# Wide attention: probabilities scaled on GpSimd before the transposes, one step later, in place of spreading the reciprocal sums through TensorE

## Chip, core and metric

The kernel runs on one core of one Trainium2 chip. The metric is the device time of one execution in microseconds (us), and the median of several executions is what counts. The engines are TensorE (PE; its weight loads are listed apart as PEld), VectorE (DVE), ScalarE (ACT), GpSimd (POOL) and SyncE (SP).

## Reference

The whole program is a network of 16 layers, each added to its input `x` of shape (4, 512, 128) after a layer norm. The change touches one of them, the wide attention `L1b`, with 16 heads of size 64 and `D` = 128:

```
q = einsum('bnd,hde->bhne', query, Wq) / sqrt(64)
k = einsum('bmd,hde->bhme', query, Wk)
v = einsum('bmd,hde->bhme', query, Wv)
attn = softmax(einsum('bhne,bhme->bhnm', q, k), axis=-1)
out = einsum('bhnm,bhme->bnhe', attn, v)
out = swapaxes(out, -1, -2).reshape(B, N, E * H)
x = x + dot(out, Wp) + bp
```

All of it is float32.

## The kernel before

A loop on the chip runs twice, each time over two batch rows (`NB` = 2) of 512 tokens (`T`), through all 16 layers. So `wide_attention` (L1446 on) runs twice in one execution. `x` lies with features on the partitions.

**Tiling.** A unit `u` is one batch row and one pair of heads: `UN` = 16 units. A step `s = 4u + t` is a tile of 128 queries of a unit, for both heads of the pair: `STEPS` = 64. PSUM has eight banks of 128x512: banks 0 to 3 take scores (two per step, alternating), bank 4 the transposes of head 0, bank 5 those of head 1, bank 6 (`SMALL`) projections, the spread sums and the output in turn, bank 7 (`PV`) the sum of the products of a unit.

**One step.** TensorE computes the scores of two heads (`scores`, L1502). VectorE takes the row maxima (`maxima`, L1635) and negates them (L1637, a 128x2 operation from SBUF to SBUF, `mneg`). ScalarE takes the exponential of each head with the row sum as a by-product (`exps`, L1598; a second short record reads the accumulator) into `pr`. TensorE turns the 128x512 probabilities of each head in four 128x128 transposes (`turn`, L1513), and VectorE (head 0, L1661) and ScalarE (head 1, L1623) copy them to `prt`. Once a unit's four steps are turned, `products(u, j)` (L1525) multiplies v by `prt`, one `j` in each step of the next unit.

**The normalisation.** After the fourth step of a unit VectorE takes the reciprocal of the eight sums (L1666, `inv`). TensorE spreads them over the partitions with eight small matmuls against the identity (`denominators`, L1536) into bank 6, ScalarE copies them to `invb` (`take_spread`, L1606), and VectorE multiplies bank 7 by `invb` into `at` (`normalise`, L1643). After eight units `output` (L1545) multiplies `at` by `Wp`: 16 records of TensorE, after which VectorE adds the result to `xs` (L1648).

**Order.** Every engine has its own instruction stream in program order, written out by hand, with semaphores between them. In step `s` TensorE runs `scores(s+1)`, `products(u-1, t)`, at t = 0 `denominators(u-1)` (and in unit 9 `output(0)`), at t = 1 to 3 one projection of unit u+2 (`project`, L1488 for k and q, L1491 for v), and `turn(s)`. The last two units have no projections left. VectorE runs `maxima(s+1)`, the copy of head 0 of step `s`, and at t = 3 the reciprocal and `normalise(u-1)`. ScalarE runs `exps(s+1)`, at t = 0 `take_spread(u-1)`, at t >= 1 the copy of a projection (`take`), and the copy of head 1. GpSimd has no work in this layer. `products(u, 0)` waits for the copies of step 4u+3 by both engines and, through `at_ready`, until bank 7 has been read for unit u-1.

Of the kernel before, what the change touches and what calls it, by code (L numbers as in the profile page):

```python
# [5 lines left out]
P = 128  # L6
BATCH = 4
T = 512
# [3 lines left out]
KT = T // P  # L12
# [5 lines left out]
HE = 64  # L18
# [5 lines left out]
ALU = mybir.AluOpType  # L24
# [1422 lines left out]
def wide_attention(g, name):  # L1447
# [5 lines left out]
    with Stage(g, name) as st:  # L1453
# [4 lines left out]
        pr = st.sb("pr", [P, 2, 2, T])  # L1458
# [3 lines left out]
        total = st.sb("total", [P, 2, KT, 2])  # L1462
        inv = st.sb("inv", [P, 2, KT, 2])
        invb = st.sb("invb", [P, T])
# [3 lines left out]
        inverse, spread, spread_in, pv, at_ready, out_ready, added = (  # L1468
            st.sem(n) for n in ("inverse", "spread", "spread_in", "pv", "at_ready", "out_ready", "added"))
        SMALL, PV = 6, 7  # L1470

        with g.nc.Block() as block:
# [5 lines left out]
            def _(pe):  # L1478
                ln.tensor(pe)

                def project(u, j):
# [3 lines left out]
                    if u >= 3 and j == 0:  # L1485
                        pe.wait_ge(spread_in, u - 2)
# [19 lines left out]
                def turn(s):  # L1506

                    for h in range(2):
                        pe.wait_ge(prob, 2 * s + h + 1)
                        if s >= 1:  # L1510
                            pe.wait_ge((turned_dve, turned_act)[h], s)
                        for j in range(KT):
                            mm = pe.transpose(g.ps[:, 4 + h, j * P:(j + 1) * P], pr[:, s % 2, h, j * P:(j + 1) * P], g.w("ident"))  # L1513
# [16 lines left out]
                def denominators(u):  # L1530

                    pe.wait_ge(inverse, u + 1)
                    pe.wait_ge(proj_in, min(3 * (u + 3), 3 * UN))
                    for t in range(KT):
                        for h in range(2):
                            mm = pe.matmul(g.ps[HE * h:HE * h + HE, SMALL, t * P:(t + 1) * P], widen(inv[:, u % 2, t, h:h + 1], HE), g.w("ident"),  # L1536
                                           start=True, stop=True, skip_group_check=True)
                    mm.then_inc(spread, 1)

                def output(b):  # L1540

                    pe.wait_ge(at_ready, PAIRS * (b + 1))
                    pe.wait_ge(spread_in, min(PAIRS * (b + 1) + 1, UN))
# [9 lines left out]
                for s in range(STEPS):  # L1553
# [3 lines left out]
                    if u >= 1:  # L1557
                        products(u - 1, t)
                    if t == 0 and u >= 1:
                        denominators(u - 1)  # L1560
                        if u % PAIRS == 1 and u > 1:
                            output(u // PAIRS - 1)
# [4 lines left out]
                    turn(s)  # L1567
                denominators(UN - 1)
# [5 lines left out]
            def _(act):  # L1574
# [14 lines left out]
                def exps(s):  # L1589

                    u, t = s // KT, s % KT
                    act.wait_ge(max_in, s + 1)
                    if t == 0 and u >= 2:
                        act.wait_ge(inverse, u - 1)
# [548 lines left out]
```

## Time and profile before

| what | us |
|---|---|
| median of three runs | 3803.88 (3800.67 to 3805.98) |
| the profiled execution | 3797.76 |
| its span | 3796.1 |

| engine | busy us in the whole span | share |
|---|---|---|
| PE | 2777.9 | 73% |
| DVE | 1910.9 | 50% |
| ACT | 1454.2 | 38% |
| POOL | 563.0 | 15% |

The layer `L1b` lies between about 639 and 929 us of the span, and in the second pass of the loop between about 2523 and 2813 us. A row of the timeline gives the start in us from the start of the span, the duration in us, the engine, the line, the operation, output <- input, the shapes and how often it stands there in a row; in square brackets is the idle time ahead of it and what ended it. Float32 matmuls are recorded as two instructions each.

### The profile page before, as it was taken

The page shows a single profiled execution, that of the slowest core. Times are in us where ns is not written, and L with a number is a line of the kernel's source. Part 1 is how long each engine was busy: PE and PEld are TensorE (multiplying, and loading weights), DVE is VectorE, ACT ScalarE, POOL GpSimd, SP SyncE. Part 2 cuts the span into 40 slices and gives each one's busy share as a digit, 9 for nine tenths or more (in the row PEclk, how much of TensorE's full clock was granted, in tenths as well). Part 3 has the DMA queues.
Part 4 walks back from the last instruction along what each step waited for, and adds up shares of the span by engine and source line. Part 5 has one row for each costly group of instructions (what it writes and reads, how often), then busy time and mean ns, then how long its engine had stood idle before and what let it go on. Part 6 is the DMA issues. An engine that isn't in the chain of part 4 may idle for free. (4 is left out here: it accounts for less than half of the span.)

```text
span 3796.1 us, 33099 instructions
## 1 busy us (share of the span) xinstructions
PE 2777.9 (73%) x11584; PEld 1230.2 (32%) x11630; DVE 1910.9 (50%) x2675; ACT 1454.2 (38%) x2370; POOL 563.0 (15%) x376
## 2 busy tenths in 40 slices
PE   3565778999695797573846567889996957965647
PEld 1221164544342343131212212635443423422312
DVE  4858642554315613872549575425533166148635
ACT  2442412654242444432434334036542423434323
POOL 0532000000014010430006400000000140105300
PEclk8897969999797998895969889599997979988969
DMA  2001000000011110002000020000000011100010
GB/s 85 0 1 42 10 1 1 1 1 1 6 39 30 23 45 0 0 3 20 1 12 0 0 44 8 1 1 1 1 1 28 17 34 18 45 0 0 9 14 6
DMA packets 103312, 52.11 MB, mean 14 GB/s; under 512 B 75232, under 2 KB 91616, under 8 KB 103136
## 3 DMA queue, kind: packets, MB, share of 16 engines
q1 hardware_dynamic: 103136, 49.88, 5.6%
q8 instruction: 96, 1.57, 0.2%
q14 instruction: 80, 0.66, 0.1%
HBM read 40.02 MB, written 9.44 MB: 13 GB/s over the span
## 5 line engine op out<-in xcount | busy, mean ns | idle before, releaser
L1598 ACT ACTIVATE L1b_pr<-ps,L1b_mneg 128x512 f32<-128x512 f32 x256 | 173.5, 683 | 196.1 <-DVE L1b_mneg L1637 196.1
L518 POOL TENSOR_TENSOR xs<-xs,L2f_part 128x512 f32<-128x512 f32 x32 | 40.5, 1265 | 1286.6 <-DVE L2f_part L507 1286.6
L1635 DVE TENSOR_REDUCE L1b_m<-ps 128x2 f32<-128x1024 f32 x128 | 156.8, 1225 | 104.9 <-PE ps L1502 100.8
L1356 ACT ACTIVATE L0b_pt<-ps 128x1024 f32<-128x1024 f32 x128 | 129.5, 1023 | 208.6 <-PE ps L1294 206.7
L90 ACT ACT_TABLE_LOAD x32 | 41.1, 1283 | 423.3 <-PEq L671 180.5
L1403 DVE TENSOR_REDUCE L0b_mx<-ps 128x1 f32<-128x512 f32 x256 | 161.3, 685 | 46.8 <-PE ps L1278 38.9
L1046 POOL TENSOR_TENSOR L0a_db<-L0a_du,L0a_bs 128x1024 f32<-128x1024 f32 x64 | 150.3, 2353 | 224.4 <-ACT L0a_bs L1017 213.7
L1046 POOL TENSOR_TENSOR L3a_db<-L3a_du,L3a_bs 128x1024 f32<-128x1024 f32 x64 | 150.3, 2352 | 224.6 <-ACT L3a_bs L1017 214.1
L1356 ACT ACTIVATE L2b_pt<-ps 128x1024 f32<-128x1024 f32 (+3 forms) x128 | 88.5, 703 | 204.8 <-PE ps L1297 204.3
L1278 PE MATMUL ps<-L0b_ks,L0b_qs 128*128 128x512 bf16 x246 | 100.7, 446 | 87.8 <-DMA L0b_ks<-parts_dram 51.9
L1661 DVE COPY L1b_prt<-ps 128x512 f32<-128x512 f32 x128 | 88.6, 692 | 124.8 <-PE ps L1513 124.5
L1122 DVE TENSOR_TENSOR_SCAN L0a_hs<-ps,L0a_db 128x1024 f32<-128x1024 f32 x64 | 146.1, 2283 | 10.0 <-ACT ps L1009 8.0
L1122 DVE TENSOR_TENSOR_SCAN L3a_hs<-ps,L3a_db 128x1024 f32<-128x1024 f32 x64 | 146.1, 2283 | 9.5 <-ACT ps L1009 8.0
L1502 PE MATMUL ps<-L1b_k,L1b_q 64*128 64x512 f32 x512 | 144.0, 640 | 0.0
L1403 DVE TENSOR_REDUCE L2b_mx<-ps 128x1 f32<-128x128 f32 (+3 forms) x256 | 116.8, 486 | 53.7 <-PE ps L1281 52.2
L116 PE MATMUL ps<-xs,weights 128*128 128x512 f32 x128 | 82.6, 780 | 78.9 <-PEq L220 27.2
L1525 PE MATMUL ps<-L1b_prt,L1b_v 128*64 128x512 f32 x512 | 136.7, 614 | 4.1 <-issue 2.0
L1513 PE MATMUL ps<-weights,L1b_pr 128*128 128x128 f32 x1024 | 135.8, 275 | 3.0 <-ACT L1b_pr L1598 3.0
L1513 PEld LDWEIGHTS ps<-weights,L1b_pr 128*128 128x128 f32 x1024 | 115.6, 141 | 50.6 <-issue 43.5
L1278 PE MATMUL ps<-L2b_ks,L2b_qs 128*128 128x256 bf16 (+3 forms) x242 | 74.8, 343 | 77.4 <-DMA L2b_ks<-parts_dram 50.9
L946 PE MATMUL ps<-L0a_hc,weights 128*128 128x512 f32 x256 | 127.7, 623 | 2.7 <-DVE L0a_hc L1127 2.7
L946 PE MATMUL ps<-L3a_hc,weights 128*128 128x512 f32 x256 | 127.4, 622 | 2.7 <-DVE L3a_hc L1127 2.7
(567 smaller groups left out, 5787.8 us busy)
## 6 DMA issues: line engine op xcount, KB each, us to landing
L2f_w<-expert_dram SPq DMA_DIRECT2D x32, 256.0 KB, 3.0
L2g_w<-expert_dram SPq DMA_DIRECT2D x32, 256.0 KB, 3.1
weights<-w_dram SPq DMA_DIRECT2D x7, 789.5 KB, 8.8
parts_dram<-L0b_cut SPq DMA_DIRECT2D x4, 768.0 KB, 3.3
L0b_qs<-parts_dram SPq DMA_DIRECT2D x96, 32.0 KB
L0b_ks<-parts_dram SPq DMA_DIRECT2D x96, 32.0 KB
parts_dram<-L2b_cut SPq DMA_DIRECT2D x4, 768.0 KB, 3.3
L2b_qs<-parts_dram SPq DMA_DIRECT2D x96, 32.0 KB
```

The costliest lines, as they stand in the source:

```text
L946: mm = pe.matmul(g.ps[:, k, :], g.w("ident"), hc[:, n % 2, k, :], start=(s == 0), stop=(s == NS - 1))
L1046: pool.tensor_tensor(db[:, n % 2, :, :], du[:, b, :, :], bcast(bs[:, n % 2, :], 1, 2), ALU.mult).then_inc(input_ready, 1)
L1122: dve.tensor_tensor_scan(flat(hs), decay_banks(n).rearrange("p k t -> p (k t)"), flat(db), 0.0, ALU.mult, ALU.add).then_inc(scanned, 1)
L1278: mm = pe.matmul(g.ps[:, 4 + a % 2, 0:span(t)], qs[:, b, i, r, t * P:(t + 1) * P], ks[:, b, i, r, 0:span(t)], start=True, stop=not causal)
L1356: act.activation(pt[:, n % 3, 2 * half:2 * half + 2, q0:T], g.ps[:, 2 * (s % 2):2 * (s % 2) + 2, q0:T], ACT.Exp).then_inc(prob, 1)
L1403: dve.tensor_reduce(mx[:, u, n:n + 1], g.ps[:, 4 + a % 2, 0:span(n % 4)], AX.X, ALU.max).then_inc(top_in, 1)
L1502: mm = pe.matmul(g.ps[:, 2 * (s % 2) + h, :], q[HE * h:HE * h + HE, u % 3, t * P:(t + 1) * P], k[HE * h:HE * h + HE, u % 3, :], start=True ...
L1513: mm = pe.transpose(g.ps[:, 4 + h, j * P:(j + 1) * P], pr[:, s % 2, h, j * P:(j + 1) * P], g.w("ident"))
L1525: mm = pe.matmul(g.ps[HE * h:HE * h + HE, PV, :], v[:, u % 4, j, HE * h:HE * h + HE], prt[:, u % 2, h, j, :], start=(j == 0), stop=(j == K ...
L1598: act.activation(pr[:, s % 2, h, :], g.ps[:, 2 * (s % 2) + h, :], ACT.Exp, bias=mneg[:, s % 2, h:h + 1], accum_out=total[:, u % 2, t, h:h ...
L1635: dve.tensor_reduce(m[:, s % 2, :], g.ps[:, 2 * (s % 2):2 * (s % 2) + 2, :], AX.X, ALU.max).then_inc(max_raw, 1)
L1661: dve.tensor_copy(prt[:, u % 2, 0, :, t * P:(t + 1) * P], g.ps[:, 4, :].rearrange("p (j c) -> p j c", c=P)).then_inc(turned_dve, 1)
```

## The change

`denominators`, `take_spread`, `normalise`, the tile `invb` and the semaphores `spread` and `spread_in` go. In their place:

- VectorE takes the reciprocal of a step's two sums in every step (`invert`), 128x2 in place of 128x8.
- GpSimd multiplies the probabilities of each head by that reciprocal, in place, in SBUF: two `tensor_scalar` of 128x512 in every step, which raise `normal`.
- `turn` waits for `normal` and no longer for `prob`, and is run one step later: `turn(s-1)` in step `s`, at the end of the step. `pr` has three buffers for it. `products` go one step later as well, so `products(u-1, 0)` stands in step 4u+1. `output` goes from t = 0 to t = 1, ahead of `project`.
- `take_at(u)` on VectorE copies bank 7 to `at` in place of `normalise`. It stands at t = 0 of unit u+2, behind `invert(s+1)`.
- `total` and `inv` alternate by step, `exps(s)` waits for `inverse` of two steps before.

```diff
-        pr = st.sb("pr", [P, 2, 2, T])
+        pr = st.sb("pr", [P, 3, 2, T])
...
# TensorE
                 def turn(s):
                     for h in range(2):
-                        pe.wait_ge(prob, 2 * s + h + 1)
+                        pe.wait_ge(normal, 2 * s + h + 1)
...
-                def denominators(u):
-                    pe.wait_ge(inverse, u + 1)
-                    pe.wait_ge(proj_in, min(3 * (u + 3), 3 * UN))
-                    for t in range(KT):
-                        for h in range(2):
-                            mm = pe.matmul(g.ps[HE * h:HE * h + HE, SMALL, t * P:(t + 1) * P], widen(inv[:, u % 2, t, h:h + 1], HE), g.w("ident"),
-                                           start=True, stop=True, skip_group_check=True)
-                    mm.then_inc(spread, 1)
...
                     if s + 1 < STEPS:
                         scores(s + 1)
-                    if u >= 1:
-                        products(u - 1, t)
-                    if t == 0 and u >= 1:
-                        denominators(u - 1)
-                        if u % PAIRS == 1 and u > 1:
-                            output(u // PAIRS - 1)
+                    if s >= 1 + KT:
+                        products((s - 1) // KT - 1, (s - 1) % KT)
+                    if t == 1 and u > 1 and u % PAIRS == 1:
+                        output(u // PAIRS - 1)
                     if t >= 1 and u + 2 < UN:
                         if t == 1 and u > 1 and u % PAIRS == 1:
                             pe.wait_ge(added, u // PAIRS)
                         project(u + 2, t - 1)
-                    turn(s)
-                denominators(UN - 1)
+                    if s >= 1:
+                        turn(s - 1)
+                products(UN - 2, KT - 1)
+                turn(STEPS - 1)
                 for j in range(KT):
                     products(UN - 1, j)
                 output(NB - 1)
# ScalarE
                     act.wait_ge(max_in, s + 1)
+                    if s >= 2:
+                        act.wait_ge(inverse, s - 1)
...
                     if s + 1 < STEPS:
                         exps(s + 1)
-                    if t == 0 and u >= 1:
-                        take_spread(u - 1)
                     if t >= 1 and u + 2 < UN:
                         take(u + 2, t - 1)
...
+                    if s >= 1:
+                        take_turned(s - 1)
+                take_turned(STEPS - 1)
# GpSimd
+                for s in range(STEPS):
+                    pool.wait_ge(inverse, s + 1)
+                    for h in range(2):
+                        pool.tensor_scalar(pr[:, s % 3, h, :], pr[:, s % 3, h, :], inv[:, s % 2, h:h + 1], None, ALU.mult).then_inc(normal, 1)
# VectorE
+                def invert(s):
+                    dve.wait_ge(prob, 2 * s + 2)
+                    if s >= 2:
+                        dve.wait_ge(normal, 2 * (s - 1))
+                    dve.reciprocal(inv[:, s % 2, :], total[:, s % 2, :]).then_inc(inverse, 1)
...
+                def take_at(u):
                     dve.wait_ge(pv, u + 1)
-                    dve.tensor_tensor(at[:, u // PAIRS % 2, u % PAIRS, :], g.ps[:, PV, :], invb[:, :], ALU.mult).then_inc(at_ready, 1)
+                    dve.tensor_copy(at[:, u // PAIRS % 2, u % PAIRS, :], g.ps[:, PV, :]).then_inc(at_ready, 1)
...
                 maxima(0)
+                invert(0)
                 for s in range(STEPS):
                     u, t = s // KT, s % KT
                     if s + 1 < STEPS:
                         maxima(s + 1)
-                    if t == 0 and u > 1 and u % PAIRS == 1:
+                    if t == 1 and u > 1 and u % PAIRS == 1:
                         output(u // PAIRS - 1)
+                    if s >= 1:
+                        take_turned(s - 1)
+                    if s + 1 < STEPS:
+                        invert(s + 1)
                     if t == 0 and u >= 2:
+                        take_at(u - 2)
...
+                take_at(UN - 2)
+                take_turned(STEPS - 1)
+                take_at(UN - 1)
                 output(NB - 1)
```

## Rows read from the trace of the kernel before

**Rows 1.** The page's first part: busy us, share and instructions of each engine.

```profile
PE 2777.9 (73%) x11584; PEld 1230.2 (32%) x11630; DVE 1910.9 (50%) x2675; ACT 1454.2 (38%) x2370; POOL 563.0 (15%) x376
```

**Rows 2.** Windows, layer `L1b`, first pass: window, us; PE, PEld, DVE, ACT, POOL; PEclk.

```profile
646.00:929.00 283.00, 271.75 (x1504) 135.88 (x1502) 145.62 (x226) 156.08 (x384) 0.00 (x0) 1.00 0.00 1
```

**Rows 3.** Timeline, a step with a projection (t = 1), 787.7 to 791.8 us.

```profile
787.78 1.13 PE L1502 MATMUL ps<-L1b_k,L1b_q 64*128 64x512 f32 x4
...
788.84 1.08 PE L1525 MATMUL ps<-L1b_prt,L1b_v 128*64 128x512 f32 x4
...
790.81 1.04 PE L1513 MATMUL ps<-weights,L1b_pr 128*128 128x128 f32 x8
...
791.45 0.69 DVE L1661 COPY L1b_prt<-ps 128x512 f32<-128x512 f32 x1 [1.06 <-PE ps L1513]
...
791.78 1.13 PE L1502 MATMUL ps<-L1b_k,L1b_q 64*128 64x512 f32 x4
```

**Rows 4.** Timeline, the step ahead of it (t = 0, with `denominators`), 783.7 to 787.8 us.

```profile
783.70 1.13 PE L1502 MATMUL ps<-L1b_k,L1b_q 64*128 64x512 f32 x4
...
784.09 0.64 DVE L1643 TENSOR_TENSOR L1b_at<-ps,L1b_invb 128x512 f32<-128x512 f32 x1
...
784.84 0.23 PEld L1525 LDWEIGHTS ps<-L1b_prt,L1b_v 128*64 128x64 f32 x4 [0.84 <-DVE L1b_prt L1661]
...
784.88 1.23 DVE L1635 TENSOR_REDUCE L1b_m<-ps 128x2 f32<-128x1024 f32 x1
...
785.75 1.07 PE L1536 MATMUL ps<-weights,L1b_inv 128*64 128x128 f32 x16
...
786.14 0.17 DVE L1637 TENSOR_SCALAR L1b_mneg<-L1b_m 128x2 f32<-128x2 f32 x1
786.34 0.69 ACT L1598 ACTIVATE L1b_pr<-ps,L1b_mneg 128x512 f32<-128x512 f32 x1 [1.61 <-DVE L1b_mneg L1637]
...
786.76 1.09 PE L1513 MATMUL ps<-weights,L1b_pr 128*128 128x128 f32 x8
...
787.59 0.20 ACT L1598 ACTIVATION_READ_ACCUMULATOR L1b_pr<-ps,L1b_mneg 128x1 f32 x1
```

**Rows 5.** Timeline, a step of the last units, with no projection: two `scores` in turn.

```profile
896.05 1.13 PE L1502 MATMUL ps<-L1b_k,L1b_q 64*128 64x512 f32 x4
...
899.14 1.13 PE L1502 MATMUL ps<-L1b_k,L1b_q 64*128 64x512 f32 x4
```

**Rows 6.** Timeline, `output(0)` in unit 9 and what follows it.

```profile
804.52 7.10 PE L1545 MATMUL ps<-L1b_at,weights 128*128 128x512 f32 x16 [1.59 <-ACT L1b_invb L1606]
...
811.46 1.04 PE L1513 MATMUL ps<-weights,L1b_pr 128*128 128x128 f32 x8
...
811.66 0.75 DVE L1648 SCALAR_TENSOR_TENSOR xs<-ps,weights,xs 128x512 f32<-128x512 f32 x1 [9.25 <-PE ps L1545]
```

**Rows 7.** Timeline, the layer's end: `scores(61)`, the last four `products`, the last addition.

```profile
902.23 1.13 PE L1502 MATMUL ps<-L1b_k,L1b_q 64*128 64x512 f32 x4
...
916.38 3.60 PE L1525 MATMUL ps<-L1b_prt,L1b_v 128*64 128x512 f32 x16
...
928.02 0.75 DVE L1648 SCALAR_TENSOR_TENSOR xs<-ps,weights,xs 128x512 f32<-128x512 f32 x1 [7.23 <-PE ps L1545]
```

**Rows 8.** Single lines on GpSimd, min/median/max in ns, first and last start.

```profile
L518 POOL TENSOR_TENSOR xs<-xs,L2f_part x32: 1260/1264/1270, 1063.3 to 3051.2; 128x512 f32<-128x512 f32 x32
...
L1375 POOL COPY L0b_vpad<-L0b_v x4: 396/858/1386, 304.1 to 306.6; 128x256 f32<-128x256 f32 x4
...
L1370 POOL MEMSET L0b_vpad<- x4: 524/524/524, 302.9 to 2188.0; 128x512 f32 x4
```

**Rows 9.** Timelines of GpSimd and VectorE in layer `L0b`, 284 to 309 us.

```profile
284.13 7.35 POOL L1365 MEMSET L0b_qs<- 128x8192 bf16 x1
...
285.92 6.11 DVE L1393 CAST L0b_cut<-L0b_ln_xc 128x1024 bf16<-128x1024 f32 x1
...
308.55 0.69 DVE L1397 CAST L0b_cut<-L0b_ln_xc 128x1024 bf16<-128x1024 f32 x1
```

More of the change, by code:

```diff
@@ L1461, in wide_attention @@
         mneg = st.sb("mneg", [P, 2, 2])
-        total = st.sb("total", [P, 2, KT, 2])
-        inv = st.sb("inv", [P, 2, KT, 2])
-        invb = st.sb("invb", [P, T])
+        total = st.sb("total", [P, 2, 2])
+        inv = st.sb("inv", [P, 2, 2])
         at = st.sb("at", [P, 2, PAIRS, T])
@@ L1467, in wide_attention @@
             st.sem(n) for n in ("proj", "proj_in", "score", "max_raw", "max_in", "prob", "turned", "turned_dve", "turned_act"))
-        inverse, spread, spread_in, pv, at_ready, out_ready, added = (
-            st.sem(n) for n in ("inverse", "spread", "spread_in", "pv", "at_ready", "out_ready", "added"))
+        inverse, normal, pv, at_ready, out_ready, added = (
+            st.sem(n) for n in ("inverse", "normal", "pv", "at_ready", "out_ready", "added"))
         SMALL, PV = 6, 7
@@ L1484, in project @@
                     pe.wait_ge(proj_in, 3 * u + j)
-                    if u >= 3 and j == 0:
-                        pe.wait_ge(spread_in, u - 2)
                     if j < 2:
@@ L1592, in exps, with take_turned @@
                     act.wait_ge(max_in, s + 1)
-                    if t == 0 and u >= 2:
-                        act.wait_ge(inverse, u - 1)
-                    for h in range(2):
-                        if s >= 2:
-                            act.wait_ge(turned, 2 * (s - 2) + h + 1)
-                        act.activation(pr[:, s % 2, h, :], g.ps[:, 2 * (s % 2) + h, :], ACT.Exp, bias=mneg[:, s % 2, h:h + 1],
-                                       accum_out=total[:, u % 2, t, h:h + 1]).then_inc(prob, 1)
-                def take_spread(u):
-                    act.wait_ge(spread, u + 1)
-                    if u >= 1:
-                        act.wait_ge(at_ready, u)
-                    act.activation(invb[:, :], g.ps[:, SMALL, :], ACT.Copy).then_inc(spread_in, 1)
+                    if s >= 2:
+                        act.wait_ge(inverse, s - 1)
+                    for h in range(2):
+                        if s >= 3:
+                            act.wait_ge(turned, 2 * (s - 3) + h + 1)
+                        act.activation(pr[:, s % 3, h, :], g.ps[:, 2 * (s % 2) + h, :], ACT.Exp, bias=mneg[:, s % 2, h:h + 1],
+                                       accum_out=total[:, s % 2, h:h + 1]).then_inc(prob, 1)
+                def take_turned(s):
+                    u, t = s // KT, s % KT
+                    act.wait_ge(turned, 2 * s + 2)
+                    if t == 0 and u >= 2:
+                        act.wait_ge(pv, u - 1)
+                    act.activation(prt[:, u % 2, 1, :, t * P:(t + 1) * P], g.ps[:, 5, :].rearrange("p (j c) -> p j c", c=P), ACT.Copy).then_inc(turned_act, 1)
                 for u in range(2):
```

31 lines of the change are left out of this document (11 added, 20 removed).

## The prediction

> **What bounds the kernel now.** I began with the page's busy shares: TensorE works 73% of the span, GpSimd 15% [rows 1]. Over the whole program that says little, since the change sits in one layer, so the second view was the windows of that layer. There TensorE is busy 271.75 of 283 us at a granted clock of 1.00 (its 2.4 GHz level), VectorE 146, ScalarE 156, GpSimd not at all [rows 2]. The layer is bound by TensorE's stream, and the same holds in the second pass. The third view was the timeline of one unit. A step with a projection lasts 787.78 to 791.78, 4.00 us, and TensorE goes from one group to the next without a wait [rows 3]. The step at t = 0 lasts 783.70 to 787.78, 4.08 us, of which 784.84 - 783.70 - 1.06 = 0.08 is a wait for the copies (1.06 is the spacing of `scores` and `products`, 787.78 to 788.84) [rows 3, 4]. A unit is thus about 16.1 us, and 16 units a pass give most of the 283 us.
>
> So work taken off TensorE's stream is worth its full length, but only as long as no wait takes its place. Where the other engines then stand has to be read at the step that is shortened.
>
> **What is removed from TensorE.** `denominators` takes the stream from 785.75 to 786.76, 1.01 us, once a unit [rows 4]. Sixteen a pass and two passes would be 32 us if nothing else came. The steps without a projection show the group `scores`, `products`, `turn` alone: 3.09 us [rows 5]. So the new step at t = 0 takes 3.09 us of work, and the other three stay at 4.00.
>
> **What TensorE then waits for.** Let 0 be the start of `scores(4u+1)`, in the step at t = 0. The next scores start at 3.09, and `products(u-1, 0)`, which the change puts behind them, could start at 3.09 + 1.06 = 4.15. It waits for `at_ready` of unit u-2, since it writes bank 7 anew. That is `take_at(u-2)`, and on VectorE it is queued behind `invert(4u+1)`, which waits for both exponentials of step 4u+1. The chain from 0, all on ScalarE and VectorE: the reduction starts at 1.18 (784.88 - 783.70), the negation at 2.44, the first exponential at 2.64, and the last accumulator read ends at 787.79, that is 4.09 [rows 4]. The reciprocal follows at 4.13 or so (the exponential starts 0.03 after the negation's end, 786.31; I take the same hand-over). Before it is a 128x8 operation followed at 0.11 us by the next on VectorE; that spacing I take for the 128x2 one. `take_at` starts at about 4.24 and lasts 0.64 to 0.69, as the multiply it replaces [rows 4] and the copy of the same size [rows 3]. With 0.05 for the hand-over TensorE can go at 4.96. That is a wait of 4.96 - 4.15 = 0.81 us in each unit. ScalarE's copy of the turned head 1, the other thing that `products(u-1, 0)` waits for, is done by 4.09 + 0.60, so it is not the last.
>
> Of 1.01 + 0.08 = 1.09 us, then, 0.81 comes back as the wait; with the small differences in spacing (4.08 + 1.06 to `products(u-1, 1)` before, 4.96 after) the gain is 5.14 - 4.96 = 0.18 us a unit. This is the step on which the forecast rests.
>
> **Whether a second wait forms.** VectorE is busy until 4.9 with `take_at`, so the maxima of step 4u+2, whose scores were there at 3.09 + 1.18 = 4.27, start 0.6 late and their exponentials end near 7.8. The next that needs them is `scores(4u+4)`, at 7.9 + 4.0; covered. The copies of the turned probabilities have over 1 us of cover. GpSimd: it gets step s at 4.09 + 0.2 after `scores(s)` and must be ready when `turn(s)` starts, a whole step later, at about 10.9 (`turn(4u+1)`). With duration p for each of the two, 4.4 + 2p < 10.9 holds for p below 3.2, and its throughput, 8p < 15.9 a unit, for p below 2.0. In the last two units, steps of 3.09, p must stay below 1.5.
>
> **The duration p** is not in the trace: there is no GpSimd `tensor_scalar`. Below stands the write alone, MEMSET of the same size, 0.524; above, the two-input TENSOR_TENSOR of the same size, 1.264. The nearest in kind reads one input and writes one output, the COPY of 128x256, 0.396 undisturbed, which doubled is 0.79 with its fixed part counted twice [rows 8]. I take 0.6 to 0.8, and keep 0.52 to 1.27. The Trainium skill, "GPSIMD Engine Reference", section Engine selection, says that one-input operations run at about line rate there; by that p would be at the low end of this range.
>
> **The other parts, one pass.** Start: the first maxima are held back by `invert(0)`, but `project` waits for ScalarE there already; worked through with the same durations, the seventh scores come 0.1 us later (0 to +1). Units 2 to 8 and 10 to 13, eleven of them: 11 x -0.18 = -2.0. Unit 9: the 1.59 us that `output(0)` waits for `invb` goes; in its place `project` stands right behind the output and waits for VectorE's addition, 811.66 - 811.46 + 0.75 + 0.05 = 1.0 us [rows 6], where a `turn` and more lay between before. So -0.6, and -0.18 as in the others: -0.8. Unit 14: -0.2. Unit 15 and the end: counted from `scores(61)`, the first products start at 4.96 and then come turn 60, scores 63, products, turn 61, products, turn 62, products, with spacings of 1.01 to 1.06, so that `turn(63)` starts at 13.15. Its 1.1 us, the ScalarE copy of 0.6 and hand-overs put the last four products at 15.05, where they start at 916.38 - 902.23 = 14.15 now [rows 7]. From there to the last addition all is as before. So +0.9. Off the path: 48 more reciprocals on VectorE, 16 copies fewer on ScalarE, both covered by TensorE.
>
> Sum: 0.1 - 2.0 - 0.8 - 0.2 + 0.9 = -2.0 a pass, two passes -3.9 us. The profiled execution, 3797.76 us with a span of 3796.1, would become 3793.9. It lies 6.1 below the median of the runs, so the forecast in terms of the median is 3803.9 - 3.9 = 3800.
>
> **Rival 1, slower: GpSimd holds up VectorE's negation.** The trace has it in another layer: a VectorE cast from SBUF to SBUF, 0.69 us when GpSimd is idle, took 6.11 us when it met a GpSimd MEMSET, and ended at 292.03, 0.55 after the MEMSET's end at 284.13 + 7.35 = 291.48 [rows 9]. It waited the instruction out. The negation `mneg` also goes from SBUF to SBUF with one input, and it is in the chain above. At t = 0 it comes at 2.44. GpSimd gets step 4u when `invert(4u)` is done. That one stands behind the copy that ends at 791.45 + 0.69 - 787.78 = 4.36 in its step [rows 3], i.e. at 0.36 of this one, so GpSimd starts at about 0.57 and ends at 0.63 + 2p. With p below 0.90 it is over by 2.44 and costs nothing. With p = 1.26 it ends at 3.15, and the negation ends near 3.26 in place of 2.61: 0.65 us in each of 14 waits a pass, 28 x 0.65 = 18 us, net +14, 3818. From p = 1.15 on it is slower by more than 0.2%. Against it: the COPY row; for it: no row shows a `tensor_scalar` as fast as a COPY. Chance 0.22, at any strength. The Trainium skill states this as a rule ("SBUF — State Buffer", section Who interferes with whom): a one-source VectorE operation in a two-port mode and a GpSimd instruction exclude each other for the whole instruction, whoever comes first; "Vector Engine (DVE) Microarchitecture Reference", section 5.1, adds that two elements a partition suffice. By that rule the trace agrees for the cast; for 128x2 no row shows it.
>
> **Rival 2, faster: the wait is not there.** If `take_at` were not last, all of the 1.01 us would be kept: 28 x 0.81 = 23 more, 27 in all, 3777. Against it stand the program order and the measured chain. Chance 0.10.
>
> **Rival 3: GpSimd becomes the bound**, from p = 2.0. With p = 2.35, a far price, a unit takes 18.8, 2.7 more than now, 28 x 2.7 = +75, 3879. Chance 0.05; the layer's TENSOR_TENSOR of 1.264 speaks against it.
>
> **How the numbers follow.** The forecast has 0.63. Its own range, from 0 to +1 at the start, 0.64 or 0.69 for the copy, 0.1 either way in the hand-overs (28 x 0.1 = 2.8) is 3795 to 3804. The range that should hold 8 in 10 goes up to rival 1 at p = 1.27, 3820, and leaves out rivals 2 and 3: 3794 to 3820. This kernel can be told from no change at about 0.2%, 7.6 us. Faster by more: rival 2 and 0.08 of the forecast, 0.18. Slower by more: rival 3, 0.15 of rival 1 and 0.03 of the forecast, 0.23. The rest, 0.59, is within.
>
> **What would show it.** In the profile after: a spacing of `scores` at t = 0 of 3.09; `products(u-1, 0)` released by VectorE's `L1b_at` with the wait of 0.8 us; a unit of 15.9 us; GpSimd at 0.6 to 0.8 each, so 256 of them busy 154 to 205 us in the two passes together; the negation still 0.17. If the negation reads 0.3 or more at t = 0, rival 1 is at work. If the products are released by ScalarE or wait for nothing, the forecast's main step is wrong; so it is if TensorE's clock leaves 1.00 in this layer.

## The result and the profile after

The changed kernel takes 3815.65 us (median of 6 runs, 3814.51 to 3820.48) against 3801.69 for the kernel before, measured beside it: a ratio of 1.0038, 95% interval 1.0025 to 1.0051. It is slower by about 14 us, where 3800 and no measurable change were forecast. The time lies inside the stated range of 3794 to 3820, but the forecast had the change at -4. The profiled execution has a span of 3814.1 us.

The page: TensorE is busy 13 us less than in [rows 1], GpSimd 393 more. The new line alone has 397, with a mean of 1.563 us.

```profile
span 3814.1 us, 32421 instructions
...
PE 2764.9 (72%) x11118; PEld 1201.8 (32%) x11118; DVE 1947.6 (51%) x2771; ACT 1438.7 (38%) x2338; POOL 956.2 (25%) x632
...
L1615 POOL TENSOR_SCALAR L1b_pr<-L1b_pr,L1b_inv 128x512 f32<-128x512 f32 x256 | 397.0, 1563 | 431.7 <-DVE L1b_inv L1635 431.7
```

The window of the layer in the first pass (window, us; PE, PEld, DVE, ACT, POOL; PEclk), which answers to [rows 2]. The clock is still 1.00; TensorE does 13.1 us less in 4 us more. Over both passes that is 26.2 us less, of which the page shows 13.0, so TensorE was busy some 13 us longer in other layers.

```profile
646.00:933.00 287.00, 258.63 (x1248) 120.39 (x1248) 163.23 (x274) 148.20 (x368) 198.52 (x128) 1.00 0.00 1
```

From one load of ScalarE's table to the next, layer `L1b` takes 290.65 us a pass before and 294.82 after. That is 8.4 of the 14 us; the rest lies in layers that the change does not touch, and has its own part below.

TensorE's waits in this layer (what waited <- for what: us in total, times, longest us). The wait that was forecast is there, once in each of 14 units, with 1.0 us on average.

```profile
PE ps L1522 <- DVE L1b_at L1648: 14.3, 14, 1.7
```

The step at t = 0 in the timeline of after (start, us, engine, line; in brackets the idle time before and its releaser), which answers to [rows 4] and the forecast chain:

```profile
786.25 1.13 PE L1499 MATMUL ps<-L1b_k,L1b_q 64*128 64x512 f32 x4
...
786.79 3.10 POOL L1615 TENSOR_SCALAR L1b_pr<-L1b_pr,L1b_inv 128x512 f32<-128x512 f32 x2 [0.91 <-DVE L1b_inv L1635]
...
788.69 0.34 DVE L1628 TENSOR_SCALAR L1b_mneg<-L1b_m 128x2 f32<-128x2 f32 x1
...
789.34 1.13 PE L1499 MATMUL ps<-L1b_k,L1b_q 64*128 64x512 f32 x4
...
790.31 0.20 ACT L1585 ACTIVATION_READ_ACCUMULATOR L1b_pr<-ps,L1b_mneg 128x1 f32 x1
...
790.63 0.67 DVE L1648 COPY L1b_at<-ps 128x512 f32<-128x512 f32 x1
...
791.45 1.08 PE L1522 MATMUL ps<-L1b_prt,L1b_v 128*64 128x512 f32 x4 [0.97 <-DVE L1b_at L1648]
```

Counted from `scores` at 786.25: the next scores at 3.09 as forecast, the negation at 2.44 as forecast but 0.34 long in place of 0.17, the last read over at 4.26 (forecast 4.09), `take_at` at 4.38 (4.24), the products at 5.20 (4.96). A unit is 16.16 us, not 15.93, and the layer's middle gains nothing (16.10 before).

The layer's end, which answers to [rows 7]. GpSimd's pairs follow each other every 3.36 us, 3.10 for the pair and 0.26 of idle time, while a TensorE step is 3.09 there:

```profile
903.11 3.10 POOL L1615 TENSOR_SCALAR L1b_pr<-L1b_pr,L1b_inv 128x512 f32<-128x512 f32 x2 [0.26 <-DVE L1b_inv L1635]
...
904.19 0.51 DVE L1628 TENSOR_SCALAR L1b_mneg<-L1b_m 128x2 f32<-128x2 f32 x1
...
904.59 1.13 PE L1499 MATMUL ps<-L1b_k,L1b_q 64*128 64x512 f32 x4
...
905.98 0.20 ACT L1585 ACTIVATION_READ_ACCUMULATOR L1b_pr<-ps,L1b_mneg 128x1 f32 x1
...
906.47 3.10 POOL L1615 TENSOR_SCALAR L1b_pr<-L1b_pr,L1b_inv 128x512 f32<-128x512 f32 x2 [0.26 <-DVE L1b_inv L1635]
...
910.47 1.08 PE L1522 MATMUL ps<-L1b_prt,L1b_v 128*64 128x512 f32 x4 [1.66 <-DVE L1b_at L1648]
...
921.75 3.65 PE L1522 MATMUL ps<-L1b_prt,L1b_v 128*64 128x512 f32 x16 [0.73 <-issue]
...
933.36 0.75 DVE L1653 SCALAR_TENSOR_TENSOR xs<-ps,weights,xs 128x512 f32<-128x512 f32 x1 [7.23 <-PE ps L1532]
```

The 3.36 us are a loop, and not what GpSimd needs for its pair. The negation is held, 0.51 us in place of 0.17, and ends 1.59 us after the pair's start at 903.11. The exponentials and their reads follow until 906.18, then the reciprocal, and GpSimd's next pair waits for that: 1.59 + 1.77 = 3.36. The same 1.77 us behind the negation's end gives the spacing in the experiments below with 256 columns (1.40 and 3.17) and with `tensor_tensor` (2.06 and 3.82). Where there is no negation to hold, the same pairs follow each other without idle time, every 3.08 us (the line is shown with the experiment that moves both copies and keeps `tensor_scalar`).

From `scores(61)` at 904.59 to the last addition it takes 28.77 us, where it took 25.79. At the start of the layer GpSimd works at the same spacing of 3.36 us from its first step on:

```profile
661.24 3.10 POOL L1615 TENSOR_SCALAR L1b_pr<-L1b_pr,L1b_inv 128x512 f32<-128x512 f32 x2 [155.32 <-DVE L1b_inv L1635]
...
664.60 3.10 POOL L1615 TENSOR_SCALAR L1b_pr<-L1b_pr,L1b_inv 128x512 f32<-128x512 f32 x2 [0.26 <-DVE L1b_inv L1635]
```

**The layer cut into its stretches**, by the starts of the `scores` groups in the timelines, first pass, in us. Start is from the first scores to `scores(9)`; the units are the mean of seven from there; unit 9 holds `output(0)`; the end is from `scores(61)` to the last addition.

| kernel | start | unit | unit 9 | unit 14 | end | layer |
|---|---|---|---|---|---|---|
| before | 31.37 | 16.10 | 24.66 | 13.35 | 25.79 | 290.65 |
| forecast | 31.5 | 15.93 | 23.9 | 13.15 | 26.7 | 288.7 |
| after | 32.44 | 16.16 | 24.14 | 13.40 | 28.77 | 294.82 |
| GpSimd 2 of 512 columns | 31.28 | 15.98 | 23.97 | 13.23 | 26.77 | 289.37 |
| GpSimd 256 of 512 columns | 31.96 | 15.99 | 23.96 | 13.23 | 27.34 | 290.70 |
| GpSimd tensor_tensor | 35.30 | 15.99 | 23.96 | 13.24 | 30.36 | 297.06 |

The differences to before, the unit taken eleven times, make up the layer: for after, 1.07 + 0.6 - 0.52 + 0.05 + 2.98 = 4.18.

### The profile page after: what moved, and what is told of

It reads as the page before. It is cut to its first block and busy times, and to the rows that moved or that the text cites. A ratio compares the mean times of both kernels' runs of the same rounds, so it can differ in the third digit from the quotient of the medians.

```text
span 3814.1 us, 32421 instructions
## 1 busy us (share of the span) xinstructions
PE 2764.9 (72%) x11118; PEld 1201.8 (32%) x11118; DVE 1947.6 (51%) x2771; ACT 1438.7 (38%) x2338; POOL 956.2 (25%) x632
## 5 line engine op out<-in xcount | busy, mean ns | idle before, releaser
L1615 POOL TENSOR_SCALAR L1b_pr<-L1b_pr,L1b_inv 128x512 f32<-128x512 f32 x256 | 397.0, 1563 | 431.7 <-DVE L1b_inv L1635 431.7
L518 POOL TENSOR_TENSOR xs<-xs,L2g_part 128x512 f32<-128x512 f32 x32 | 40.5, 1266 | 494.9 <-DVE L2g_part L507 494.9
L1278 PE MATMUL ps<-L2b_ks,L2b_qs 128*128 128x128 bf16 (+3 forms) x256 | 79.8, 346 | 79.5 <-DMA L2b_ks<-parts_dram 52.8
L946 PE MATMUL ps<-L3a_hc,weights 128*128 128x512 f32 x256 | 128.9, 628 | 2.7 <-DVE L3a_hc L1127 2.7
```

What stands on the lines that cost most here:

```text
L946: mm = pe.matmul(g.ps[:, k, :], g.w("ident"), hc[:, n % 2, k, :], start=(s == 0), stop=(s == NS - 1))
L1278: mm = pe.matmul(g.ps[:, 4 + a % 2, 0:span(t)], qs[:, b, i, r, t * P:(t + 1) * P], ks[:, b, i, r, 0:span(t)], start=True, stop=not causal)
L1615: pool.tensor_scalar(pr[:, s % 3, h, :], pr[:, s % 3, h, :], inv[:, s % 2, h:h + 1], None, ALU.mult).then_inc(normal, 1)
```

## The experiments

Ratios are to the kernel before, run on the same chip; "the layer" is `L1b` a pass. Theory: the wait at t = 0 is as forecast, and GpSimd's duration costs the rest. First rival: the structure of the change costs it, whatever GpSimd does.

**GpSimd scales 2 of 512 columns** (the other probabilities stay unscaled).

```diff
-pool.tensor_scalar(pr[:, s % 3, h, :], pr[:, s % 3, h, :], inv[:, s % 2, h:h + 1], None, ALU.mult)
+pool.tensor_scalar(pr[:, s % 3, h, 0:2], pr[:, s % 3, h, 0:2], inv[:, s % 2, h:h + 1], None, ALU.mult)
```

> The kernel after, with GpSimd scaling only 2 of the 512 columns of each head, so the rest of the probabilities stays unnormalised; semaphores and order as in after. It takes away GpSimd's duration (1.56 us each) and with it both its hold on the negation and its being the bound in the last units. Theory A (GpSimd is all that separates the result from the forecast): negation back at 0.17 us, products(u-1,0) 4.96 us after scores(4u+1) in place of 5.20, a unit 15.93 in place of 16.16, L1b about 288.7 us a pass, 2 us under before, ratio to before 0.999. Theory B (the forecast's sum was wrong in its main step, GpSimd does not matter): unit stays 16.16 and L1b 294.8, ratio 1.003 to 1.004.

Measured: 3800.49 us, ratio 0.9990 (0.9981 to 0.9999); the layer 289.37. The step at t = 0:

```profile
781.94 1.13 PE L1499 MATMUL ps<-L1b_k,L1b_q 64*128 64x512 f32 x4
...
784.37 0.17 DVE L1628 TENSOR_SCALAR L1b_mneg<-L1b_m 128x2 f32<-128x2 f32 x1
...
786.14 0.67 DVE L1648 COPY L1b_at<-ps 128x512 f32<-128x512 f32 x1
...
786.96 1.08 PE L1522 MATMUL ps<-L1b_prt,L1b_v 128*64 128x512 f32 x4 [0.80 <-DVE L1b_at L1648]
```

The negation is back at 0.17, the products start at 5.02, the unit is 15.98. This is the forecast's own case of a cheap GpSimd, and each of the five stretches in the table comes within 0.25 us of the forecast's (the unit within 0.05, which counts eleven times). The 5.45 us a pass between this kernel and after, 10.9 in all, are the price of GpSimd's duration. The structure alone was worth 1.3 us a pass.

**GpSimd scales 256 of 512 columns** (the other half stays unscaled), the same edit with `0:256`.

> The changed kernel with GpSimd scaling only the first 256 of each head's 512 probability columns (the other half stays unscaled). Its duration, linear between 0.287 us at 2 columns and 1.563 at 512, would be 0.92, and GpSimd is done before the negation in the step at t = 0. Theory (only the duration was missed): a unit of 15.98 as with 2 columns, the layer 289.4 to 290.5 a pass, no wait for GpSimd in the last two units, 3800 to 3803. Rival (GpSimd's presence costs whatever its duration, through the start and the end of the layer): the layer above 292, 3807 or more.

Measured: 3801.6 us, ratio 1.0005 (0.9996 to 1.0014); the layer 290.70, 0.2 above the theory's range and far from the rival's. The GpSimd group of the layer (busy us, mean ns):

```profile
L1615 POOL TENSOR_SCALAR L1b_pr<-L1b_pr,L1b_inv 128x256 f32<-128x256 f32 x128 | 116.9, 925 | 292.9 <-DVE L1b_inv L1635 292.9
```

With 0.925 us the layer is level with the kernel before (290.70 against 290.65): near this duration the change as made breaks even in its layer. The unit is 15.99 as with 2 columns, so what is left of the price stands at the start (0.7) and the end (0.6).

**The negation in the reduction**, so that no VectorE instruction stands between the maxima and the exponentials that GpSimd could hold.

```diff
-dve.tensor_reduce(m[...], ps, AX.X, ALU.max)
-dve.wait_ge(max_raw, s + 1)
-dve.tensor_scalar(mneg[...], m[...], -1.0, None, ALU.mult)
+dve.tensor_reduce(mneg[...], ps, AX.X, ALU.max, negate=True)
```

> The kernel after with the negation of the row maxima done by the reduction itself (its negate option, source PSUM), so that the 128x2 VectorE operation from SBUF to SBUF is gone. Theory A (GpSimd held up that operation: 0.36 us in the middle in place of 0.17, up to 0.59): the chain at t = 0 loses the operation and its hold, 0.34 + 0.04 us, so products(u-1,0) starts 4.8 us after scores(4u+1) in place of 5.20, 14 x 0.38 = 5.3 us less a pass, L1b 289 to 290, ratio to before 0.999 to 1.000. Theory B (the longer negation is only how it is recorded, no hold): only its own 0.17 + 0.04 goes, 14 x 0.2 = 2.9 a pass, L1b 292, ratio 1.001.

Measured: 3803.77 us, ratio 1.0006 (0.9997 to 1.0015); the layer 286.31, 8.5 below after. Its step at t = 0:

```profile
851.89 1.13 PE L1499 MATMUL ps<-L1b_k,L1b_q 64*128 64x512 f32 x4
...
853.07 1.22 DVE L1626 TENSOR_REDUCE L1b_mneg<-ps 128x2 f32<-128x1024 f32 x1 [0.74 <-PE ps L1499]
...
856.71 1.08 PE L1522 MATMUL ps<-L1b_prt,L1b_v 128*64 128x512 f32 x4 [0.59 <-DVE L1b_at L1646]
```

The products start at 4.82, 0.38 earlier than in after: 0.17 of it is GpSimd's hold, the rest the negation's own 0.17 and a hand-over of 0.04. The unit is 15.78. The gain is larger than the 289 to 290 expected, because the start gains 2.0 us and the end 1.6: there the negation was held longer (0.5 us in place of 0.17), and each step waits for it.

**The same in the kernel before**, as a fair base. The edit is the same three lines.

> The kernel before, with the negation done inside the reduction (negate) and the separate VectorE instruction gone. Theory: in the kernel before TensorE waits only 0.08 us a unit for a copy behind the exponentials, so 0.2 us off that chain gives at most 16 x 0.08 = 1.3 and a little in the first and last steps: the layer 288.5 to 290.6 a pass (290.65 before), 3797 to 3801. Rival (the negation is worth as much here as it was in the changed kernel, 8.5 us a pass): 3785.

Measured: the layer 289.64, as the theory has it. The negation is worth 1.0 us here against 8.5 in the changed kernel: 0.6 at the start (30.76), 0.2 in unit 9, 0.2 at the end, and nothing in the other units (16.11). In the units it is on the path in the changed kernel alone. The whole, however, took 3816.06 us, ratio 1.0040 (1.0027 to 1.0053), 16 slower, in layers that the edit doesn't touch. Neither theory had that; it is taken up below.

**GpSimd by `tensor_tensor`**, the reciprocal read with a stride of zero.

```diff
-pool.tensor_scalar(pr[:, s % 3, h, :], pr[:, s % 3, h, :], inv[:, s % 2, h:h + 1], None, ALU.mult)
+pool.tensor_tensor(pr[:, s % 3, h, :], pr[:, s % 3, h, :], widen(inv[:, s % 2, h:h + 1], T), ALU.mult)
```

> The kernel after with GpSimd's tensor_scalar replaced by a tensor_tensor with the reciprocal read at stride 0 as second input. Theory A (a tensor_scalar with a pointer is slow on GpSimd, two inputs are not): each takes 1.26 us in place of 1.56, as the two-input row of the trace of before; in the last two units, where steps are 3.09 us, GpSimd (2.6 a step) is no longer the bound, so the end of L1b is 2 us earlier; the negation at t = 0 meets it less, 0.1 us in 14 waits. L1b 291 to 293, ratio 1.000 to 1.002. Theory B (the duration is set by in-place work or by meeting VectorE): it stays at 1.5 or more and L1b at 294.8.

Measured: 3809.49 us, ratio 1.0021 (1.0012 to 1.0030). GpSimd takes 1.041 us each, a third less, and the units fall to 15.99, yet the layer is 297.06, longer than with the slower form and outside what either theory has. The timeline at the layer's start shows why:

```profile
659.45 2.04 POOL L1615 TENSOR_TENSOR L1b_pr<-L1b_pr,L1b_inv 128x512 f32<-128x512 f32 x2 [155.29 <-DVE L1b_inv L1635]
...
660.53 0.99 DVE L1628 TENSOR_SCALAR L1b_mneg<-L1b_m 128x2 f32<-128x2 f32 x1
...
663.27 2.04 POOL L1615 TENSOR_TENSOR L1b_pr<-L1b_pr,L1b_inv 128x512 f32<-128x512 f32 x2 [1.78 <-DVE L1b_inv L1635]
664.38 0.96 DVE L1628 TENSOR_SCALAR L1b_mneg<-L1b_m 128x2 f32<-128x2 f32 x1
...
667.36 1.47 PE L1485 MATMUL ps<-xn,weights 128*128 128x512 f32 x2 [3.18 <-ACT L1b_k L1574]
...
668.62 1.92 PE L1510 MATMUL ps<-weights,L1b_pr 128*128 128x128 f32 x8
```

The negation of 0.17 us takes 0.99 and ends at 661.52, 0.03 after GpSimd's second instruction (659.45 + 2.04). The exponentials wait for the negation, the reciprocal for them, GpSimd for the reciprocal, and the next maxima stand behind it on VectorE, so that GpSimd's next pair meets the next negation again: a closed loop of 3.82 us a step (659.45, 663.27, 667.10), where TensorE needs 3.09. Behind TensorE's wait of 3.18 us the granted clock falls: it reads 0.67 for 667 to 670 us, a part of it at the lower level of 1.2 GHz, and the eight transposes take 1.92 in place of 1.04.

```profile
667.00:670.00 3.00, 2.64 (x9) 1.82 (x10) 2.41 (x4) 1.60 (x5) 2.04 (x2) 0.67 0.00 0
```

The same loop runs again at the layer's end. This is the hold of rival 1 in full; in after the loop runs as well, with a shorter hold and 3.36 us a step.

**VectorE takes at(u-2) ahead of the reciprocal at t = 0.**

```diff
+if t == 0 and u >= 2: take_at(u - 2)
 if s + 1 < STEPS: invert(s + 1)
-if t == 0 and u >= 2: take_at(u - 2)
```

> The changed kernel with one move: in the steps at t = 0 VectorE takes at(u-2) ahead of the reciprocal of step s+1. Theory (two queues hold products(u-1,0), VectorE's take_at and, right beside it, ScalarE's copy of the turned head 1 behind the exponentials of step s+1): the products then wait for ScalarE, whose last accumulator read ends 4.09 + 0.17 = 4.26 us after scores(4u+1) and whose copy takes 0.6, so they start at about 4.9 in place of 5.20: a unit of 15.9 instead of 16.16, the layer some 3 us a pass shorter than the 294.8 of the changed kernel, 291 to 292, and 3808 to 3811 in all. Rival (VectorE's queue alone holds them): a unit of 15.2, the layer near 282, 3790.

Measured: 3805.91 us, ratio 1.0017 (1.0008 to 1.0026); the layer 289.41, the unit 15.82. The layer is 1.6 us below the theory's range: the end came 1.0 us earlier too (27.80), which the theory did not have. The releaser changed as the theory says (counted from the scores at 783.40, the products now start at 4.85):

```profile
783.40 1.13 PE L1499 MATMUL ps<-L1b_k,L1b_q 64*128 64x512 f32 x4
...
786.77 0.68 DVE L1648 COPY L1b_at<-ps 128x512 f32<-128x512 f32 x1
...
787.56 0.59 ACT L1594 ACTIVATE L1b_prt<-ps 128x512 f32<-128x512 f32 x1
...
788.25 1.08 PE L1522 MATMUL ps<-L1b_prt,L1b_v 128*64 128x512 f32 x4 [0.63 <-ACT L1b_prt L1594]
```

`at` is taken 1.0 us earlier, and ScalarE's copy, queued behind the exponentials, holds the products almost as long.

**Both ahead**: the same, and ScalarE's `take_turned(s - 1)` ahead of `exps(s + 1)` at t = 0.

> The kernel after with two moves at t = 0: VectorE runs take_at(u-2) ahead of invert(s+1), and ScalarE runs the copy of the turned head 1 ahead of exps(s+1). Theory A (what gives back the 1.01 us of denominators is that products(u-1,0) waits behind the exponentials of step 4u+1, on both engines): the wait goes, products(u-1,0) starts 4.15 us after scores(4u+1), a unit takes 15.1 us in place of 16.16, 28 x 1.05 = 29 us less than after, about 3786, ratio to before 0.996. Theory B (VectorE, ScalarE or GpSimd with 8 x 1.56 = 12.5 us a unit hold the loop anyway): the wait turns up at scores or turn, a unit stays near 16, ratio 1.003.

Measured: 3786.05 us, ratio 0.9948 (0.9936 to 0.9959); the layer 281.27, the unit 15.16. The products start 4.19 after the scores, and wait for nothing:

```profile
778.39 1.13 PE L1499 MATMUL ps<-L1b_k,L1b_q 64*128 64x512 f32 x4
...
781.59 0.60 ACT L1594 ACTIVATE L1b_prt<-ps 128x512 f32<-128x512 f32 x1 [2.16 <-PE ps L1510]
781.76 0.68 DVE L1650 COPY L1b_at<-ps 128x512 f32<-128x512 f32 x1
...
782.58 1.08 PE L1522 MATMUL ps<-L1b_prt,L1b_v 128*64 128x512 f32 x4
```

So the work removed from TensorE, 1.01 us, is worth 0.94 us a unit once both queues let it through, even with GpSimd at 1.56.

**The kernel before with 1 of the 8 matmuls of `denominators` kept** (`range(KT)` and `range(2)` to `range(1)`, so most of the reciprocals are not spread): what the removed work alone is worth, with nothing put in its place.

> The kernel before with 1 of the 8 matmuls of denominators; the other 7 are left out, so most of the attention is scaled by stale numbers. All waits and copies stay. Theory A (TensorE's stream is the bound of before): 7/8 of 1.01 us less in each of 32, 28 us, ratio 0.9926. Theory B (a wait takes its place in before too: products(u,0) already waits 0.08 us for the copies, and the copies follow the exponentials): the step at t = 0 stays at 4.08 or loses only part, ratio 0.996 or more.

Measured: 3784.67 us, ratio 0.9949 (0.9933 to 0.9966); the layer 280.76, the unit 15.42; in unit 9 `output(0)` waits 2.3 us for `invb`, where it waited 1.6. The time lies between the two theories. The step at t = 0 shows why:

```profile
781.50 0.38 PE L1536 MATMUL ps<-weights,L1b_inv 128*64 128x128 f32 x2
781.81 1.09 PE L1513 MATMUL ps<-weights,L1b_pr 128*128 128x128 f32 x8
```

The one matmul that is kept holds the stream for 0.31 us, not for an eighth of 1.01. So 0.70 us were removed, and the unit is 0.69 shorter: what is taken off TensorE's stream comes back in full, as theory A has it, but less was taken off than it reckoned.

**Both copies ahead, GpSimd at 2 of 512 columns** (the rest unscaled).

> The changed kernel with both copies taken ahead at t = 0 and GpSimd scaling 2 of 512 columns (the rest of the probabilities stays unscaled), negation kept. Theory (removed work is worth its full length once neither queue holds the products and GpSimd costs nothing): units of 15.1, the start as before, the end without waits: 290.65 - 13 x 1.0 - 0.6 = 277 a pass, 276 to 278.5. Rival (a further wait, of a kind not seen so far, takes part of it): above 280.

Measured: 3782.16 us, ratio 0.9949 (0.9936 to 0.9962); the layer 277.88, the unit 15.17. Against the kernel with the full duration, 281.27, GpSimd still costs 3.4 a pass: 0.9 at the start, 0.6 in unit 14 and 1.9 at the end, and none of it in the units before.

**Both copies ahead and the negation in the reduction, `tensor_scalar` kept.**

> The changed kernel with both copies taken ahead at t = 0 and the negation in the reduction, but GpSimd's tensor_scalar kept, 1.56 us. Theory (GpSimd's duration then counts only where its steps are short: 3.36 us against 3.09 in the last two units, and at the start): units of 15.15 as with the faster form, the layer longer than its 276.7 by 2 to 3 at the end and 1 at the start, 279.5 to 281. Rival (with both queues cleared the duration costs nothing): 276.7. The whole is judged by this layer; the rest of the program adds 3215 to 3237.

Measured: 3776.33 us, ratio 0.9935 (0.9922 to 0.9948); the layer 279.68, the unit 15.16, the end 29.43. The start is 29.56. GpSimd's first ten instructions in the layer, where after has pairs every 3.36 us, and the last products:

```profile
659.19 15.42 POOL L1617 TENSOR_SCALAR L1b_pr<-L1b_pr,L1b_inv 128x512 f32<-128x512 f32 x10 [155.12 <-DVE L1b_inv L1635]
...
903.06 5.35 PE L1522 MATMUL ps<-L1b_prt,L1b_v 128*64 128x512 f32 x16 [0.73 <-issue]
```

The five pairs follow without idle time, 3.08 us each. So the duration alone keeps up with a step of 3.09, and the 3.36 us that the expectation takes over from after are not GpSimd's own.

**All four together** (both ahead, the negation in the reduction, `tensor_tensor`).

> The kernel after with all three: both moves at t = 0, negation in the reduction, tensor_tensor on GpSimd. If the losses are separate and TensorE is then the bound: the start and the end lose GpSimd's part, the units stay at 15.1 us, L1b 277 to 279 us a pass against 281.3 with the moves alone and 290.6 before, about 3780, ratio 0.993 to 0.994. If something else holds the loop at 15.1 (the serial chain of VectorE and ScalarE), L1b stays above 281, ratio 0.995.

Measured: 3774.11 us, ratio 0.9921 (0.9908 to 0.9935); the layer 276.66, the unit 15.17, the end 26.40. It beats both kernels, by 27 us the one before. Without a negation to hold, the faster `tensor_tensor` is the better form. Its 3.0 us a pass against the kernel ahead of it lie at the layer's end (29.43 - 26.40); the start is the same, 29.56. Of the 3.0 us GpSimd's duration makes 1.3, by which the last products start later. The other 1.7 are TensorE's clock: in the kernel ahead of it the last products take 5.35 us at a granted clock of 0.68, in part the 1.2 GHz level; in this one they take 3.65 at 1.00. TensorE had waited 0.67, 0.83 and 0.73 us shortly before them. The window of the kernel ahead (us; PE, PEld, DVE, ACT, POOL; PEclk):

```profile
903.06:908.41 5.35, 5.35 (x16) 1.73 (x16) 0.00 (x0) 0.00 (x0) 0.00 (x0) 0.68 0.00 0
```

**Repeats, and the layers that nothing touches.** The two kernels unchanged, run again:

> The kernel before, unchanged, profiled once more. Layer L1b took 290.6 us from its table load to the next layer's in the profile before, and 294.8 in the one after (+4.2 in each pass, 8.4 together), while the span grew by 18.0. The other 9.6 us lie in layers that the change does not touch (L2b, L2g, L3a, the start). Theory 1 (scatter): this second profile shows L1b within 0.1 us of 290.6 and the sum of the other layers away from the first profile by several us. Theory 2 (the change lengthens other layers, by code loading or GpSimd's state): the other layers repeat within 2 us. Ratio 1.000 either way.

> The kernel after, unchanged, measured and profiled once more. Layer L1b is 4.2 us longer in each pass, 8.4 in all, but the median lay 14 above that of before. Theory 1 (the rest is scatter of the other layers and of the measurement): L1b again 294.8 us, this median nearer to before + 8.4 than to before + 14, ratio 1.002 to 1.003. Theory 2 (the change lengthens other layers by 5 to 6 us): ratio 1.0035 to 1.0045 again, and the profile again shows layers L2b and L3a longer.

Measured: 3800.4 (ratio 0.9994, 0.9985 to 1.0004) and 3815.42 (1.0035, 1.0023 to 1.0047). The 14 us repeat. In the second profiles the layer takes 290.66 and 294.90 us, and the rest of the span 3216.4 and 3223.3, against 3214.8 and 3224.5 in the first: it repeats within 2 us in each kernel, and is 7 to 10 us longer in the changed one, as theory 2 has it in both cases. By the medians it is 5.6 us. To see whether these come from the shift in time, the kernel before was made longer in the layer:

```diff
-for t in range(KT):
+for t in [*range(KT)] * (2 if u in (3, 5, 9, 11) else 1):
```

> The kernel before, in which the eight matmuls that spread the reciprocals are issued twice in 4 of the 16 units, with the same result: TensorE's stream in this layer grows by 4 x 1.01 = 4.0 us a pass, to 294.7, about what the change adds, and nothing else is touched. Theory A (the later layers' granted clock goes by when they begin): they show the pattern of the changed kernel, 62.7 us instead of 60.5 in the first layer after, 175.8 instead of 174.6, and the total rises by 8 + 5 = 13 us, 3814. Theory B (it goes by what this layer's engines did, GpSimd's work above all): the later layers keep their times, and the total rises by 8, 3809.5.

and the negation in the kernel before was run once more:

> The kernel before with the negation done in the reduction, a second time. Its wide attention layer came 1.0 us a pass shorter, but the whole came 16 longer, in layers that the edit doesn't touch. Theory A (the rest of the program has a time of its own in each kernel, through the granted clock): 3812 to 3820 again, the rest 12 us or more above that of the kernel before. Theory B (the rest varies from run to run and from chip to chip alone): 3797 to 3804.

Measured: the longer kernel 3817.81 us (3805.99 to 3824.12), ratio 1.0049 (1.0036 to 1.0062), its layer 294.15, so 7.0 us of its 17.7 are explained; the negation kernel 3808.41 us, ratio 1.0017 (1.0008 to 1.0025), in place of 3816.06, which is between the ranges of its two theories. Windows over `L2a`, the second layer behind `L1b` (the first, `L1g`, takes 48.4 us in every run), the same instructions in all four: before, after, the negation kernel, the longer one.

```profile
977.45:1037.97 60.52, 31.27 (x108) 19.36 (x108) 26.30 (x70) 16.13 (x37) 0.00 (x0) 0.71 0.00 1
```

```profile
982.80:1045.55 62.75, 33.34 (x108) 21.02 (x108) 26.29 (x70) 16.13 (x37) 0.00 (x0) 0.67 0.00 0
```

```profile
977.35:1039.65 62.30, 33.10 (x108) 20.57 (x108) 26.29 (x70) 16.13 (x37) 0.00 (x0) 0.66 0.00 0
```

```profile
981.38:1042.13 60.75, 31.52 (x108) 19.47 (x108) 26.29 (x70) 16.13 (x37) 0.00 (x0) 0.71 0.00 1
```

VectorE, ScalarE and the counts agree; only the granted clock, a mean over stretches at its two levels, and TensorE's times differ. The negation kernel enters the layer 0.1 us from where before does and has the longer form; the longer kernel enters it 1.4 us from where after does and has the shorter. Theory A falls for this layer. In the profiled execution of the longer kernel, the fastest of its five, the rest of the span is 3216.0 us, as theory B has it; by the median of the five it is not. The median without twice the layer (median - 2 x layer) is 3220 us for before, 3226 for after, and in the others lies between 3215 (`tensor_tensor`) and 3237 (the negation kernel, 3229 when run again), in no order of the layer's length or of GpSimd's work.

Nor do the 5.6 us stand in `L2a`: in after the next layer, `L2f`, gives its 2.2 us back (128.4 us against 130.6 before). So some 6 of the 14 us of this change lie in layers that it does not touch, and the rest of the program differed by -5 to +17 us over the kernels here. That the granted clock makes the whole of it is argued from `L2a` and not shown, and what sets that clock stays open. The verdicts above therefore go by the layer, whose two passes agree within 0.03 us in each kernel.

## Why the prediction was wrong

**What bounds the kernel, and the work removed**: right. Scores at t = 0 follow at 3.09; the removed work is worth 0.94 us a unit where nothing else holds the products.

**The wait that takes its place**: right, in place, releaser and size. With GpSimd made cheap it is 0.80 us (forecast 0.81) and the unit 15.98 (15.93); the 0.05 is the hand-over from VectorE to TensorE, 0.15 in the trace, for which 0.05 was taken. ScalarE's copy was "not the last", but by only 0.35 us: moving VectorE's copy alone brings 0.34 us a unit, moving both 1.0. A small misreading changes nothing: the 0.08 us of wait before the products at t = 0 is read at their weight load, and the matmul itself starts 0.03 later.

**The duration p**: the step that failed. It was taken at 0.6 to 0.8 and bounded at 1.27 by the two-input TENSOR_TENSOR [rows 8], as if one input could not cost more than two. It measured 1.563 us at 512 columns, 0.925 at 256, 0.287 at 2. The bound was of another instruction, and no row excluded more. The Trainium skill, "GPSIMD Engine Reference", section Engine selection, has one-input operations at about line rate; here the form with a scalar read per partition, 1.563 us, is slower than the two-input form of layer `L2f`, 1.264, and the measurement decides. With p outside its bounds, all that hung on it moved: the start +1.07 (forecast +0.1) and the end +2.98 (+0.9). It did not come by the condition that the prediction names for the end ("in the last two units, p must stay below 1.5"). That limit is 3.09 / 2 = 1.545, and pairs without idle time take 3.08 us, so GpSimd just keeps up there. It came through the hold of rival 1.

**Rival 1**: the mechanism was right, and most of p's price came by it, some 3.5 of the 5.45 us a pass before the layer's end is reached (13 x 0.18 in the units, 1.16 at the start); the prediction priced it in the wrong place. The negation read 0.34 at t = 0, the mark set for it, and costs 0.17 of the 0.24 us by which the products came later than forecast. The price was not: held to the end of the pair it would have been at 0.63 + 2 x 1.56 + 0.11 = 3.86 and cost 1.25 us a unit. With `tensor_scalar` it ended at 788.69 + 0.34 - 786.79 = 2.24 after the pair's start, and the pair ran for 0.86 more. What the prediction did not work through is where no step of TensorE covers the hold: at the start and the end, where negation, exponentials, reciprocal and GpSimd form a loop of 3.36 us. At the start the hold is all of the price: without a negation the start is 29.56 us with 1.56 and with 1.04 alike. At the end no run parts the hold from GpSimd's own duration; once the scores are over, `turn` also waits for GpSimd there.

**Start, unit 9, unit 14, end**: with GpSimd cheap -0.09, -0.69, -0.12, +0.98 against +0.1, -0.8, -0.2, +0.9. These terms stand; their sum with the units is -1.3 a pass, where -2.0 was forecast.

**The whole**: layer +4.17 a pass, of it -1.3 structure and +5.45 GpSimd, twice. The other 5.6 us lie in layers that the change does not touch; the prediction had no term for them, and their cause stays open. Rival 2 (no wait) needs both copies moved, and then holds: 3786 with these two moves, 3774 with the other two edits as well. Rival 3 did not come: its condition on the throughput of a whole unit (p = 2.0) was not reached, nor was that of the last units. That the time lies inside the range is luck in part: the range ended at 3820 for rival 1 at p = 1.27 in 28 waits, and neither that duration nor that price is what came.

## What to carry to other kernels

An upper bound for an instruction that the trace doesn't have must come from its own form, or be left open, and a hold must be priced at every place where the held instruction stands on the path, not only at the one step that was studied: here the steps without cover, at the start and the end of the layer, cost the most. When work is taken off the bounding engine, ask which buffer its next group writes anew, and take all the copies that free it ahead of the long dependent work on their queues; one of two brought 0.34 us, both 1.0. And read a change by the layer it touches, as here one instruction less made a layer 1.0 us shorter and the program 6 to 16 longer.

## What the hardware showed that was not expected

- GpSimd's `tensor_scalar` with one scalar for each partition, in place, 128x512 f32: 1.563 us; `tensor_tensor` with the second input at stride zero: 1.041; two full inputs: 1.264 [rows 8]. By columns, 2, 256 and 512: 0.287, 0.925, 1.563.
- VectorE's 128x2 negation is held by both. Under `tensor_tensor` it ended 0.03 us after the pair's end (0.99 us in place of 0.17), which agrees with the whole-instruction rule of the Trainium skill, "SBUF — State Buffer", section Who interferes with whom; under `tensor_scalar` it ended either 0.02 us after the end of the pair's first instruction (1.59 us after the pair's start), or 0.70 us into the second and 0.86 before its end (2.24), and with the latter the rule does not agree. Why the forms differ wasn't tried.
- Layer `L2a`, with the same instructions, ran at granted clocks of 0.66 to 0.71 from kernel to kernel. It kept to its kernel's value in both passes (60.5 and 60.6 us before, 62.75 and 62.73 after) and in a second profile (60.6 and 62.75; the negation kernel 62.3 both times).
